# Attention, normalisations and gated experts on one core: a new order for the score products and values, a shorter ramp, rows copied directly, and exponentials over two banks

## What is computed

```python
# first layer: attention over the tokens, 8 heads of 8 channels
q, k, v = (x_seq @ W.T + bias, split into heads)
attn = softmax(einsum('bhnd,bhmd->bhnm', q, k) * dh ** -0.5)
out = einsum('bhnm,bhmd->bhnd', attn, v) @ Wo.T + bo
x = group_norm(out) * gn_w + gn_b + x
# then, over the tokens
t = t + linear_attention_4_layers(layer_norm(t))
t = t + experts_top_2_of_8(layer_norm(t))
```

## Time and profile before

| what | us |
|---|---|
| median of 3 runs | 276.88 (274.16 to 278.69) |
| the profiled execution, its own time | 272.94 |
| its span, first to last instruction | 271.1 |
| TensorE busy | 250.7 (92%) |
| VectorE busy | 194.0 (72%) |
| ScalarE busy | 179.5 (66%) |
| GpSimd busy | 47.1 (17%) |
| mean granted clock of TensorE | 0.994 |

### The profile page before, as it was taken

The page is one execution under the profiler, slowest core; times in us unless marked ns, Lnnn a source line. Parts: engine busy times, 40 slices in busy tenths (PEclk is TensorE's granted clock), DMA queues, the critical chain, the costliest instruction groups (busy, mean ns, idle before and its releaser), DMA issues.

```text
span 271.1 us, 5554 instructions
## 1 busy us (share of the span) xinstructions
PE 250.7 (92%) x2077; PEld 115.9 (43%) x2078; DVE 194.0 (72%) x283; ACT 179.5 (66%) x374; POOL 47.1 (17%) x82
## 2 busy tenths in 40 slices
PE   8999896999999999999999999998886998789895
PEld 6454332333333333333334333333333885558421
DVE  3799884799999999999899899860004752248753
ACT  2817456688898898888898888887862221128620
POOL 8960367001001011010030010010000000000351
PEclk9999998899999999999999999999999999999999
DMA  4045100423203113412000000000000000000002
GB/s 126 1 173 123 22 0 4 152 88 102 63 21 83 53 31 94 125 76 82 2 2 2 5 1 5 2 2 4 4 0 0 2 0 2 0 0 2 1 0 77
DMA packets 6330, 10.41 MB, mean 38 GB/s; under 512 B 2256, under 2 KB 3888, under 8 KB 6176
## 3 DMA queue, kind: packets, MB, share of 16 engines
q1 hardware_dynamic: 6304, 10.07, 12.5%
HBM read 7.21 MB, written 2.74 MB: 37 GB/s over the span
## 4 chain that ended last, share of the span: by engine, by line
PE 80%; DVE 9%; POOL 4%; ACT 3%; issue 2%; DMA 1%; DVEq 0%; SPq 0%; POOLq 0%
PE psum L487 25%; PE psum L431 16%; PE psum L403 16%; PE psum L707 3%; DVE negmax L1037 2%; PE psum L460 2%; ACT probs L883 2%; PE psum L616 2%; PE psum L368 1%; PE psum L625 1%; POOL kop L743 1%; POOL qop L743 1%; PE psum L688 1%; PE psum L453 1%; PE psum L374 1%
## 5 line engine op out<-in xcount | busy, mean ns | idle before, releaser
L1037 DVE TENSOR_REDUCE negmax<-psum 128x1 f32<-128x1024 f32 x128 | 153.1, 1223 | 17.5 <-PE psum L403 16.0
L883 ACT ACTIVATE probs<-psum 128x512 f32<-128x512 f32 x256 | 138.0, 596 | 22.6 <-PE psum L431 15.2
L431 PE MATMUL psum<-qop,kop 64*128 64x512 f32 x256 | 93.3, 452 | 3.3 <-ACT probs L883 3.1
L403 PE MATMUL psum<-kop,qop 64*128 64x512 f32 x256 | 93.6, 448 | 2.0 <-DVE negmax L1037 1.8
L487 PE MATMUL psum<-probs,v_aug 128*32 128x256 f32 x1024 | 80.2, 392 | 0.0
L403 PEld LDWEIGHTS psum<-kop,qop 64*128 64x128 f32 x256 | 38.6, 185 | 30.6 <-DVE negmax L1037 16.4
L431 PEld LDWEIGHTS psum<-qop,kop 64*128 64x128 f32 x256 | 38.2, 185 | 30.8 <-ACT probs L883 19.1
L487 PEld LDWEIGHTS psum<-probs,v_aug 128*32 128x32 f32 x1024 | 21.2, 108 | 40.4 <-ACT probs L883 25.1
L785 POOL TENSOR_TENSOR attn<-o_tok,rden 128x64 f32<-128x64 f32 x15 | 4.5, 297 | 113.1 <-DVE rden L1028 113.1
L838 POOL TENSOR_TENSOR early<-probs,early 128x512 f32<-128x512 f32 x5 | 6.4, 1271 | 61.5 <-ACT probs L974 61.5
L497 PE MATMUL psum<-cbf_sb 128*128 128x256 bf16 x124 | 14.8, 272 | 0.0
(11 more groups left out here) (175 smaller groups left out, 193.7 us busy)
## 6 DMA issues: line engine op xcount, KB each, us to landing
parts_scratch<-early SPq DMA_DIRECT2D x4, 512.0 KB, 3.3
qop<-parts_scratch SPq DMA_DIRECT2D x28, 64.0 KB
vt_sb<-in_vt SPq DMA_DIRECT2D x1, 1024.0 KB, 4.7
kop<-parts_scratch SPq DMA_DIRECT2D x14, 64.0 KB
kop<-parts_scratch SPq DMA_DIRECT2D x28, 32.0 KB
x_sb<-in_x SPq DMA_DIRECT2D x2, 256.0 KB, 2.8
q_pair<-in_q_pairs SPq DMA_DIRECT2D x1, 512.0 KB, 4.0
qop<-max_scratch SPq DMA_DIRECT2D x28, 4.0 KB
```

The source lines that it names most:

```text
L403: last = nc.tensor.matmul(psum[:, 2 * (v % 2) + c, :], qop[at, b * PP + pp, qh * NH + t * P:qh * NH + (t + 1) * P], kop[at, b * PP + pp, c ...
L431: nc.tensor.matmul(psum[:, bank, :], kop[at, b * PP + pp, mt * P:(mt + 1) * P], qop[at, b * PP + pp, qh * NH:(qh + 1) * NH], start=True, s ...
L883: last = nc.scalar.activation(probs[:, n % P_RING, h, :], psum[:, bank, :], ACT.Exp, scale=SCALE)
L1037: V.tensor_reduce(negmax[:, i, h * HT + t:h * HT + t + 1], psum[:, bank:bank + 2, :].rearrange("p a n -> p (a n)"), AX_X, ALU.max, negate= ...
```

## The change

- **Order of the settled part.** Pairs are numbered p, four to a run. After every third pair (`PHASE`) `values` are done up to the half unit p - 4 (`VALUES_LAG`), which is one and a half units each time. A half unit is 128 of the 256 columns of the four products. At the end of a block the goal is cut there, and the next one catches up. The small work stands at such places too (`small_jobs`).
- **Ramp.** The runs with two units of maxima more are 0 and 1, so there are two units fewer ahead, and 7 runs (57 to 63) without maxima. The products of queries and keys of the first batch and of `v` stand later, those of the second batch in run 0. GpSimd zeroes `v_aug` in two halves, the second behind `eye_rep`, and TensorE waits for `eye_rep` alone.
- **Rows.** The maxima lie in `max_part` and `max_row` by head, so that SyncE copies them from `max_row` directly into `qop`. The tensor in DRAM and its wait are gone. The transpose stands at the end of a run, one run later.
- **End.** In the runs without maxima both products of a unit go to two neighbouring banks (pairs 0-1, 2-3 and 4-5), and ScalarE takes one exponential of 1024 columns. The pairs 0-1 and 2-3 are the slots of the maxima, so the first two such units wait for the last two maxima.

```diff
+PAIRS_OF = 2 * TOGETHER
+PHASE = 3
+VALUES_LAG = 4
-CATCH_UP = (1, 2, 3)
+CATCH_UP = (0, 1)
+WIDE_BANKS = (0, 2, 4)
+WIDE_SMALL = 6
...
+            if p % PAIRS_OF == PAIRS_OF - 1 if wide else ends_phase(p):
+                block_end = 2 * TT * (goal // (2 * TT) + 1)
+                goal = max(0, min(block_end, 2 * TOGETHER * (p // PAIRS_OF) if wide else p - VALUES_LAG))
+                values_goal[p] = goal
...
-                sp.dma_start(max_dram[i], max_row[:, i % 2, :]).then_inc(S["max_out"], 16)
-                sp.wait_ge(S["max_out"], 16 * (i - DIRECT + 1))
-                rows = max_dram[i].rearrange("(s i t) n -> i s (t n)", s=SPLIT, i=2)
                 for h in range(2):
                     at = HEAD_AT * h + TOP_ROW
                     sp.dma_start(qop[at:at + SPLIT, b * PP + pp, qh * NH:(qh + 1) * NH].bitcast(F32),
-                                 rows[h]).then_inc(mrow_in[i % 2], 16)
+                                 max_row[h * SPLIT * HT:(h + 1) * SPLIT * HT, i % 2, :]).then_inc(mrow_in[i % 2], 16)
...
+                elif h == 0:
+                    bank = st_free(("unit", u, 0))
+                    if bank < 4:
+                        pe.wait_ge(S["slot_free"], UNITS - (1 - bank // 2))
...
                     scores(*s[0])
                     if g:
                         max_half(jobs[0], 0)
+                    after_pair(p)
                     scores(*s[1])
                     if g:
                         max_half(jobs[0], 1)
-                    if g:
-                        values(TOGETHER * (g - 1))
+                    after_pair(p + 1)
                     max_half(jobs[1], 0)
                     scores(*s[2])
+                    after_pair(p + 2)
                     max_half(jobs[1], 1)
                     scores(*s[3])
+                    after_pair(p + 3)
...
-            nc.gpsimd.memset(v_aug[:], 0.0).then_inc(S["pool_chain"], 1)
-            pool.wait_ge(S["pool_chain"], 2)
+            pool.wait_ge(S["pool_chain"], 1)
+            nc.gpsimd.memset(v_aug[:, 0:TT // 2, :, :, :], 0.0).then_inc(S["pool_chain"], 1)
...
+                if kind == "unit":
+                    act.wait_ge(S["pv_done"], n - P_RING + 1)
+                    last = nc.scalar.activation(probs[:, n % P_RING, :, :], psum[:, bank:bank + 2, :], ACT.Exp, scale=SCALE)
```

More of the change, by code:

```diff
@@ L761, in _ @@
             pool.wait_ge(S["v_ready"], 1)
-            chain = [6]
+            chain = [3]
             def link(ins):
@@ L905, in _ @@
                 last.then_inc(S["st_done"], 1)
[L906 to L909 removed]
+                if q in copies_behind:
+                    copy_output(copies_behind[q])
             copy_output(LAST)
```

206 lines of the change are left out of this document (131 added, 75 removed).

## The result

The changed kernel takes 287.06 us (median of 4 runs, 284.55 to 289.43). The kernel before, run beside it on the same chip, takes 275.52 (median of 4, 272.95 to 278.69). The ratio is 1.042, with a 95% interval of 1.027 to 1.057: slower. The forecast was 281.4 and its range 272 to 289. The profiled executions are 289.43 (span 287.7) and 272.94 (span 271.1), so 16.5 us have to be found where the forecast had 4.5. The medians are only 11.5 apart, because the profiled execution of the changed kernel is the slowest of its four and that of the kernel before the fastest of its four.

The account below looks back on a forecast made before the run. TensorE was taken to bound the settled part, with VectorE having slack. Ramp -0.4, settled part +12.2 and end -7.3 sum to +4.5 on the profiled 272.94: 277.4, and 281.4 us for the median; range 272 to 289.

Parts of the forecast that it names:

- The settled part: From maximum 30 to the last maximum's end: 139.8 us instead of 127.6, so +12.2.
- The chain: Settled part: release, split unit's products with values between, two maxima; 4.19 us for three units, where before took 3.69.
- half units cost whole ones: Rival on values: 128 columns take as long as 256, 0.215 more in each of 35 chains, 288.9 us; chance 0.15.
- The batching pays: Rival on the settled part: the chain doesn't bind, blocks take 9.6, -9.8 there, 259.4 us in all; chance 0.12.
- the small work that lengthens the chain: Settled part from unit 30: transposes, reciprocals and places with half or two units of values add 3.4 us.
- The ramp: Up to maximum 30: its start at 52.9 instead of 53.31, so -0.4, with 1.5 either way.
- I add 5.3 of stalls: Ramp, on top of twenty maxima: 0.7 products of `v`, 1.3 first scores, 1.6 second batch, 0.9 extra units, 0.8 first split.
- The start: Ramp's beginning: TensorE's small products 0.2 earlier, another 0.2 from two products moved; maximum 0 starts at 10.2.
- The end: Stretch behind the last maximum: three pairs of banks and wide exponentials at 0.91 make it 14.8 instead of 22.1, -7.3.
- The end doesn't shorten: Rival on the end: TensorE still waits for banks in each run, -2.6 instead of -7.3, 286.1 us; chance 0.08.
- The rows: Maxima rows copied directly: a hidden 1.3 us write goes, worth nothing; lost cover would cost at most 1.3 per block.
- Slower: Sign for the whole kernel: second and fourth rivals and some 0.2 of the forecast, chance 0.43.

Follow-up runs that it names:

- run 0: Not a follow-up run: the kernel's own run numbered 0, of four pairs, in the ramp; the changed kernel puts the second batch's products there. No measured time of its own.
- e8: Kernel with the old ramp; four pairs, two whole units of values, two pairs, one unit in turn, no unit of maxima split: 272.22 us, ratio 0.997.
- e12: Old ramp, values as in the changed kernel, but from run 2 the second half of a unit's maxima comes ahead of the values: 272.47 us, ratio 0.997.
- e3: Changed kernel with the maxima from unit 30 on taken over the first 512 of 1024 keys only: 273.73 us, measured once.
- e5: e4 with the output transpose two pairs later, apart from the transpose of maxima: 266.20 us, ratio 0.973.
- e7: Changed kernel with the old order of first products and old GpSimd zeroing; catch-up and second batch stay as changed: 284.58 us, ratio 1.037.
- e2: Changed kernel with the ramp of before (first products, zeroing, catch-up in runs 1 to 3, second batch in runs 1 and 2): 281.84 us, ratio 1.032.
- e1: Changed kernel with values back behind every second pair, one whole unit each (PHASE 2, lag 3): 275.89 us, ratio 1.009.
- e4: Changed kernel with the edits of both e1 and e2, direct rows and wide exponentials left: 269.54 us, ratio 0.990.
- e6: Changed kernel with idle products in run 0 and ahead of it, into a bank nobody reads: 287.04 us, ratio 1.039.
- e9: e6 with 64 more idle products in runs 1 and 2, ahead of the maxima's products: 285.67 us, ratio 1.047.
- e10: e5 with two exponentials of 512 columns in place of each wide one, on the same banks: 266.94 us, ratio 0.977.
- e11: e5 with the rows of the maxima going through DRAM again, as in the kernel before: 266.30 us, ratio 0.976.

## Why the prediction was wrong where it was, and right where it was

**The settled part, forecast +12.2, measured +14.3.** The mechanism was right. The chain was 4.19 by working and is 4.20 in the trace. Half a unit of values costs 0.21 (a record of 0.43 beside 0.64 for a whole one), so "half units cost whole ones" is out. "The batching pays" is out by the chain (e8 and e12, each over 7 us less without the split), and e3's 128.3 shows that it would not have paid with a lighter chain either, the small work being where it is. That rival rested on a rule of the Trainium skill ("TensorEngine Tiling (Array Packing)", Key Properties), by which a change of tiling mode drains the engine. No run contradicts the rule, but saving a third of the changes saved nothing: e5 has one change for every two pairs and the shortest settled part of all kernels with the new end and full maxima. What was mis-sized is the small work that lengthens the chain, 2.1 us in the stretch. I had counted the output's transposes and those of the maxima one by one at their prices of the earlier trace rows, and their waits for a bank, 4.0 us of TensorE's idle time in the stretch, at nothing. How much of the 4.0 lengthened the chain isn't shown. A block takes 11.63 (four turns of three blocks take 139.6), against 11.2 for 8/3 chains: 0.44 a block, or 5.4 over 12.25 blocks, where my count was 3.4. The gap of 0.88 at 126.54, beside 0.60, is one with an output's transpose in the split unit.

**The ramp, forecast -0.4, measured +7.6.** This is the step that failed. The prediction said that a maximum 30 after 54.5 makes it wrong; it came at 60.92. By parts, from VectorE's timeline:

| stretch | before | forecast | after | e7 | e2 | e1 | e4 |
|---|---|---|---|---|---|---|---|
| start of maximum 0 | 10.6 | 10.2 | 12.9 | 11.0 | 10.4 | 9.8 | 10.6 |
| maxima 0 to 10 | 11.8 | 13.3 | 13.3 | 11.8 | 11.8 | 13.3 | 11.8 |
| maxima 10 to 20 | 13.9 | 14.6 | 20.2 | 18.2 | 15.3 | 17.4 | 13.0 |
| maxima 20 to 30 | 17.0 | 14.8 | 14.5 | 15.5 | 15.3 | 13.5 | 13.6 |

Two of the four rows came out as worked: the stalls at the products of `v` and ahead of the first scores, 2.0, are there in each kernel with the new start (13.3 in after, e1, e3, e6 and e9) and fall to 0.5 with the old one; and VectorE's long idle time of 2.87 is gone, by which the last row falls from 17.0 to 14.5. But the reason given for that, the earlier padding, isn't needed: the row is 13.6 in e4 and 15.3 in e2, which pad as before. The failure is "I add 5.3 of stalls" for the middle row: the 1.6 around the second batch and the 0.9 and 0.8 behind it were priced at 2.4 GHz. The sum held neither the wait that the crowding brings, TensorE idle in run 1 because VectorE is full and few values are ready, nor the half clock that follows. Nor did it hold enough for the phases of three pairs: of the 5.6 us by which the middle row is over the forecast, 2.8 go when the pairs come in twos again (e1, 17.4), where I had 0.8 for the first split unit. From maximum 0 to maximum 30 the four kernels form a square: 48.0 after, 44.3 with pairs in twos, 42.4 with the old ramp, 38.4 with both (e4). So the phases cost 3.8 to 4.0 us there and the new ramp 5.6 to 5.9, on top of a base that is 4.3 under the 42.7 of before.

In the kernel before the two products of the second batch came at 28 and 34 where the clock was 1.00, and it dropped only at 46. The trace of before had a warning, in slices of 2 us:

```profile
44.00:46.00 2.00, 0.47 (x3) 0.35 (x5) 0.00 (x0) 0.15 (x1) 1.79 (x4) 1.00 0.00 0
46.00:48.00 2.00, 2.00 (x14) 0.53 (x14) 1.17 (x1) 1.20 (x3) 0.06 (x1) 0.50 0.02 4
```

TensorE is busy for 0.47 of 2.00, and behind that its clock is 0.50. I read the gap as a price of its own and not of the clock. But such a gap doesn't always bring a fall. e5 has the like at the same place and keeps its clock:

```profile
44.00:46.00 2.00, 0.57 (x9) 0.13 (x7) 1.45 (x2) 1.08 (x2) 1.80 (x4) 1.00 0.04 8
46.00:48.00 2.00, 2.00 (x23) 0.77 (x22) 0.67 (x1) 1.21 (x3) 0.28 (x1) 1.00 0.01 2
```

e10, which has the same ramp, falls to 0.50 in 46 to 48, and maxima 20 to 30 take 15.4 us in it and 13.9 in e5: one such fall costs some 1.5. How the 5.6 us divide between clock and order isn't settled. e9's 2.5 for maxima 16 to 20 is shown, and for maxima 10 to 16 the nearest pair is after with 12.8 at half clock and e7 with 9.4 at full clock for most of it.

**The start.** Maximum 0 was forecast at 10.2. With the new start it came at 9.80, 10.18, 10.25, 11.13 and 12.91 in five profiled executions, with the old one between 10.35 and 11.40. In the latest one, that of the changed kernel, six of the chunk products took 4.43 us, and 2.82 in before, e1, e6 and e9, though the records grant the clock in full there; why is open. One execution can't tell a gain of 0.4 here, and 2.3 of the 7.6 us are of this kind. The ratios of 1.042 for after, 1.037 for e7 and 1.032 for e2 suggest that the start and the crowding of run 0 cost about the same, but both steps lie inside the intervals and so aren't shown.

**The end, forecast -7.3, measured -5.4.** The price of a wide exponential, 0.91 from one to the next, and of the record, 1.02, were right (two in 1.94 and 1028 ns); the sum behind the 1.02 was loose, since 0.390 and 0.596 extended in a line give 1.01. The Trainium skill's figures ("ScalarE: Activation LUTs", What ACT_TABLE_LOAD costs) give 1.039 for the record and, an estimate, 0.95 for the step, so here the step is shorter. Without ScalarE's 2.27 us of idle behind the four units of values the stretch would be 14.4, against 14.8. What was missed is that the change of goals at the first wide run leaves four units at once, and that the clock falls in them: 3.60 us for work that takes 1.93 where no clock is lost (1.07 + 0.86). "The end doesn't shorten" is out.

**The rows, forecast 0.** Right, by e11. The later transpose of the maxima, which the prediction counted here as harmless, stands in the kernels with the old ramp that reach maximum 30 earlier than before (e5).

**The whole.** "Slower" was the less likely of two sides that I held nearly equal (0.43, and 0.45 for the same). The profiled executions differ by 12.0 us more than forecast: 8.0 in the ramp, the one term whose sign I took for granted, 2.1 in the settled part and 1.9 in the end. With the ramp as forecast the rest, +8.5, would still be over the forecast's +4.5. That 287.06 lies inside 272 to 289 is partly luck: the top of the range stood for half units at the price of whole ones, which is out, and the ramp term was off by far more than its own 1.5 either way.

## What to carry to other kernels

When an edit lets the bounding engine catch up early, ask what the clock-gated engine does meanwhile: idle time on TensorE was in several kernels here (before, after, e7), though not in all (e5), followed by 3 to 10 us at half its clock, just where its work became the bound. Don't put other work between the two halves of something that fills a scarce slot; count a slot from the first write to the last read. And take a change apart before it is dropped: its end, its rows and its later transpose of the maxima, with the old ramp, the old rhythm and two transposes kept apart, are 2.7% faster than the kernel before, while the whole is 4.2% slower.

## What the runs showed that I had not expected

- Two small transposes of 0.37 and 0.20 us cost 0.82 when they stand together, and 3.1 us over the kernel, because both need a bank of the same ring that ScalarE frees one exponential at a time: TensorE is idle for 2.2 us ahead of the second in e4 and for none in e5.
- With VectorE's maxima halved (e3) the order with three pairs in a row still leaves TensorE idle 6.6 of 121 us, and all of it ahead of the transposes: small work that shares the scores' ring of three banks can cost as much as the batching saves.
- Idle products (e9) held the clock at 1.00 all through the ramp and saved 2.5 us in one place, but the kernel isn't faster for it: 4.7% over the kernel before, where the changed kernel is 4.2%.
- The same kernel without a fall of the clock is several us faster: e6 took 282.73 us at a mean clock of 1.00 and 286.09 to 289.08 at 0.98.
